# wqk in four transfers with four semaphores, and 24 products of zeros in place of 28

## The chip, the cores and the metric

The kernel runs on one core of a Trainium2 chip: TensorE (matrix products), VectorE, ScalarE, GpSimd, and SyncE (SP), whose queue issues most of the transfers. The metric is the device time of one execution in microseconds, as the median of several runs. Lower is better.

## The reference

Input x has 8 sequences of 512 rows of 256 numbers, in f32. First comes an attention layer that only yields one number for a row, the sum of its exponentials, and a small gate network behind it; then a layernorm; then a mixture of 12 experts, in which each row uses the best 3 in each of two layers; then a layernorm.

```python
q = (x @ Wq.T).astype(bfloat16); k = (x @ Wk.T).astype(bfloat16)
q, k = rope(q), rope(k)
e = where(causal, exp(q @ k.T / 16), 0)
o = relu(e.sum(-1) @ fc1_w.T + fc1_b) @ fc2_w.T + fc2_b
x = layernorm(x + o)
xa = x @ P_w.T;  C1, C2, C3 = softmax of the top 3 of xa @ U.T, for three U
h = gelu(sum_e C1[:, e] * (x @ W1[e].T))
y = sum_e C2[:, e] * (h @ W2[e].T) + C3 @ b2
x = layernorm(x + y)
```

## The kernel before

Every engine has its own hand-written program, and semaphores order them. The work has two stages.

The first stage goes over the rows in 8 chunks of 512 (four sequences of 128 rows each). For each chunk TensorE makes four projections, numbers g = 0 to 3: two halves of q and two of k. A projection (`project`, L767 to L776) multiplies the part `wqk[:, k, g, :]` by the transposed chunk, in f32, over two halves k; each of its two products is shown as two MATMUL records in the trace, so a projection has four. Two banks take turns, so projection n waits for the copy of projection n - 2 (L771). ScalarE copies each projection out of its bank (`qk_copy`, L561), VectorE turns it by the rope (L1078 to L1086), TensorE makes the scores of the chunk before (L786, L788), ScalarE takes exponentials and their sums (L571). Between these, parts of the second stage are prepared: the split of the experts' weights into two f16 halves, the first layernorms and the routing of the first rows. The split needs the largest absolute value of each weight array: VectorE takes that of w1T (L1092), ScalarE sums the absolute values of w2T in three parts (`w_sum`, L578). The first of these sums stands in ScalarE's program behind chunk 1, ahead of the copies of chunk 2, and waits for both parts of w2T (L577).

The second stage goes over 32 tiles of 128 rows with the experts' products (L935), most of the run's length.

At the start, GpSimd clears `zeros`, and TensorE makes `WARM` products of it that nobody reads (L957 to L958), waits for wqk (L959) and enters the loop over chunks. `project(c, 0)` also waits for its chunk's two transfers (L770). After `project(0, 1)` TensorE waits for all six small constant loads (L965) and makes the product of the routing matrices (L967).

Transfers: SP's queue issues, in this order, chunk 0 of x transposed (two transfers, L329), the routing matrices (L342, L343), chunk 1, b2 (L345), w1T in two parts (L338, L339), chunk 2, w2T in two parts (L338, L339), chunk 3, and later the rest and x's own rows (L334). ScalarE's queue issues wqk as one transfer (L548), then, behind a wait for GpSimd's clearing and one small Exp that loads its table (L550), the constants `cb`, `identf`, `iota12`, `gatew` (L551 to L554). Chunk 0 lies in memory in runs of 128 numbers (512 bytes), wqk as one transfer in runs of 4 KB for a partition.

Of the kernel before, what the change touches and what calls it, by code (L numbers as in the profile page):

```python
# [81 lines left out]
def build(nc, x, xT, wqkT, gate, fc2, p_w, uT, w1T, w2T, b2e, constb, constf, out):  # L82
    ctx = ExitStack()
    with ctx:
        def sb(name, shape, dt):
            return ctx.enter_context(nc.sbuf_tensor(name, shape, dt))
# [4 lines left out]
        def sem(name):  # L91
            return ctx.enter_context(nc.semaphore(name))
# [12 lines left out]
        wqk = sb("wqk", [P, NC, 4, P], F32)  # L105
# [69 lines left out]
        RING, HT = 4, 4  # L175

        LAST_SCORE = (HGT, MISC)
        WARM = 28
        Z = GT * NR * NE
        KEPT = 10  # L180

        ld_qk = sem("ld_qk")
        ld_const = sem("ld_const")
        ld_rows = sem("ld_rows")
        ld_b2 = sem("ld_b2")
# [81 lines left out]
        def wait(eng, s, value):  # L267

            if value > 0:
                eng.wait_ge(s, value)  # L270
# [7 lines left out]
        for i in range(NT + 2):  # L278
            order = [(i - 2, 1, j) for j in range(experts_of(i - 2))] if i >= 2 else []
            order += [(i, 0, j) for j in range(experts_of(i))] if i < NT else []  # L280
            for key in order:
                slot[key] = len(taker)
                act = key[1] == 0 and key[2] == 0
# [101 lines left out]
        def _(pool):  # L385
# [69 lines left out]
            def select_of(g):  # L455
                pool.wait_ge(ids_done, g + 1)
                pool.wait_ge(C_done, g + 1)
                _, v = nc.values_load_multi_w_load_instructions(
                    ids[0:1, g, :, :].rearrange("p m r -> p (m r)"), engines=[ENGINE.Pool], min_val=0, max_val=NE,
                    skip_runtime_bounds_check_because="an id is a sum of one-hot entries times 1..12")  # L460
                t = slice(max(GT * g, 1), GT * (g + 1))
                for m in range(NM):
                    for j in range(TOPK):
                        c = pool.tensor_copy(Csel[:, t, m, j:j + 1], C[:, t, m, bass.ds(v[REC * m + j], 1)])
                c.then_inc(csel_done, 1)
# [79 lines left out]

        @block.scalar
        def _(act):
            act.dma_start(wqk[:, :, :, :], wqkT).then_inc(ld_qk, 16)  # L548
            act.wait_ge(zero_done, 3)
            act.activation(warm[:, :], minus_half[0:1, 0:1], ACT.Exp)  # L550
            act.dma_start(cb[:, :], constb).then_inc(ld_const, 16)  # L551
# [214 lines left out]
        def _(pe):  # L766
            def project(c, g):  # L767
                n = 4 * c + g
                if g == 0:
                    pe.wait_ge(ld_seq[c % 4], 32 * (c // 4 + 1))  # L770
                wait(pe, qk_copied, n - 1)  # L771
                for k in range(NC):
                    mm = pe.matmul(bank[PROJ[n % 2]][:, :], wqk[:, k, g, :],  # L773
                                   xTb[:, c % 4, k, :, :].rearrange("p s n -> p (s n)"),
                                   start=(k == 0), stop=(k == NC - 1))
                mm.then_inc(proj_done, 1)  # L776
# [171 lines left out]
            def load_ids(g):  # L948
                pe.wait_ge(ids_done, g + 1)
                _, v = nc.values_load_multi_w_load_instructions(  # L950
                    ids[0:1, g, :, :].rearrange("p m r -> p (m r)"), engines=[ENGINE.PE], min_val=0, max_val=NE,
                    skip_runtime_bounds_check_because="an id is a sum of one-hot entries times 1..12")
                held_ids[g] = v


            pe.wait_ge(zero_done, 1)
            for n in range(WARM):  # L957
                pe.matmul(bank[SCORE[n % 2]][:, 0:DIM], zeros[:, 0:P], zeros[:, :], start=True, stop=True)  # L958
            pe.wait_ge(ld_qk, 16)  # L959
            for c in range(NCH):  # L960
                project(c, 0)
                early_aux(c, 0, early)
                project(c, 1)
                if c == 0:
                    pe.wait_ge(ld_const, 16 * 6)  # L965
                    for k in range(NC):
                        mm = pe.matmul(bank[MISC][:, k * NR * NE:(k + 1) * NR * NE], pws[:, k, :], uTs[:, :],  # L967
                                       start=True, stop=True)
                    mm.then_inc(M_done, 1)
                if c == 3:  # L970
                    peak_transpose()
                early_aux(c, 1, early)
                if c:
                    scores(c - 1, 0)
                project(c, 2)
                early_aux(c, 2, early)
                if c:
                    scores(c - 1, 1)
                project(c, 3)
                if c == 3:  # L980
                    peak_spread()
                early_aux(c, 3, early)
                if c:
                    gate_transpose(c - 1)
# [503 lines left out]
```

## Time and profile before

| | us |
|---|---|
| median of 3 runs | 300.6 |
| lowest and highest | 300.32, 302.5 |
| the profiled execution's own time | 304.48 |
| its span, first to last instruction | 302.5 |
| TensorE products busy | 271.4 (90%) |
| VectorE busy | 248.2 (82%) |
| ScalarE busy | 164.1 (54%) |
| GpSimd busy | 144.3 (48%) |

Times in the rows are microseconds from the span's start. A busy TensorE is not one at its peak, since products overlap in the records. "PEld" is the load of the stationary operand. "SPq" and "ACTq" are the queues of SP and ScalarE, on which transfers are issued. Idle time in brackets is that of the engine just ahead of the row, with what ended it.

### The profile page before, as it was taken

Reading aid. Unit: us, or ns where it says so; the run is one execution under the profiler, and the core shown is the slowest. Engines: PE = TensorE matmul, PEld = TensorE weight load, DVE = VectorE, ACT = ScalarE, POOL = GpSimd, SP = SyncE. Lnnn points to the kernel's source line nnn. Section 1 sums busy time; section 2 is a strip of 40 time slices with the busy share of each in tenths; the row PEclk is TensorE's granted clock in tenths of the full one; section 3 lists DMA queues with packets and bytes.
Section 4 is the critical chain, followed back from the end, with each engine's and each line's share of the span. In section 5 each row is a group of like instructions: output and inputs, shape, how many; then the busy total and the mean of one; then the engine's idle time right before and its main releaser. Section 6 shows DMA issues by size and latency. Waiting matters only on the chain.

```text
span 302.5 us, 6418 instructions
## 1 busy us (share of the span) xinstructions
PE 271.4 (90%) x2028; PEld 196.4 (65%) x2030; DVE 248.2 (82%) x728; ACT 164.1 (54%) x341; POOL 144.3 (48%) x315
## 2 busy tenths in 40 slices
PE   7997999997959974999999999999999999999980
PEld 5443444553526663797877877777778878788960
DVE  0368498999966985879999999999999989987872
ACT  1246745765736446036746846837846946545430
POOL 0200006999998752432482383374364362474421
PEclk9999899999979995799999999999999999999997
DMA  8997999970000000001001001000100101010111
GB/s 234 419 386 265 165 190 202 144 101 0 0 1 2 1 2 0 0 2 37 20 20 36 20 18 32 23 20 21 31 25 18 37 20 36 20 35 22 36 35 39
DMA packets 19211, 20.50 MB, mean 68 GB/s; under 512 B 1620, under 2 KB 18408, under 8 KB 18664
## 3 DMA queue, kind: packets, MB, share of 16 engines
q1 hardware_dynamic: 18456, 19.13, 26.7%
q10 hardware_dynamic: 720, 0.93, 1.0%
q8 instruction: 18, 0.29, 0.4%
q14 instruction: 17, 0.14, 0.1%
HBM read 15.83 MB, written 4.19 MB: 66 GB/s over the span
## 4 chain that ended last, share of the span: by engine, by line
PE 57%; DVE 24%; issue 7%; SPq 4%; DMA 4%; ACT 2%; POOL 0%; DVEq 0%; POOLq 0%
PE bank L935 37%; PE bank L773 8%; DVE early L1303 7%; DMA W<-in_w2T 4%; PE bank L821 4%; SPq L338 2%; DVE early L1360 2%; DVE xsin L1079 2%; PE bank L786 2%; DVE top L1172 2%; DVE zrest L1187 2%; PE bank L832 2%; DVE st L1355 1%; DVE x1T L1162 1%; DVE xcos L1078 1%
## 5 line engine op out<-in xcount | busy, mean ns | idle before, releaser
L935 PE MATMUL bank<-W,early 128*128 (+1 forms) x630 | 75.7, 276 | 5.3 <-DVE early L1360 5.3
L935 PE MATMUL bank<-W,x1T 128*128 (+1 forms) x630 | 74.9, 273 | 0.6 <-DVE early L1303 0.3
L935 PEld LDWEIGHTS bank<-W,early 128*128 128x128 f16 x630 | 60.3, 99 | 17.1 <-DVE early L1360 7.0
L935 PEld LDWEIGHTS bank<-W,x1T 128*128 128x128 f16 x630 | 59.8, 98 | 11.3 <-issue 2.5
L1303 DVE SCALAR_TENSOR_TENSOR early<-bank,Csel,early 128x256 f32<-128x256 f32 x124 | 59.7, 482 | 8.1 <-PE bank L935 3.7
L773 PE MATMUL bank<-early,wqk 128*128 128x512 f32 x128 | 63.2, 627 | 2.8 <-ACT qk L561 1.9
L773 PEld LDWEIGHTS bank<-early,wqk 128*128 128x128 f32 x128 | 23.2, 197 | 24.3 <-issue 21.8
L682 ACT ACTIVATE early<-early 128x256 f32<-128x256 f32 x32 | 13.3, 417 | 45.1 <-DVE early L1303 44.9
L561 ACT ACTIVATE qk<-bank 128x512 bf16<-128x512 f32 x32 | 18.9, 594 | 34.3 <-PE bank L773 34.2
L519 POOL TENSOR_SCALAR ve<-mv 128x1 f32<-128x1 f32 x32 | 7.3, 227 | 60.5 <-DVE mv L1356 59.9
L1078 DVE TENSOR_TENSOR xcos<-qk,cb 128x1024 bf16<-128x1024 bf16 x16 | 11.9, 746 | 20.3 <-ACT qk L561 20.2
L732 ACT ACTIVATE early<-bank,ipow 128x256 f16<-128x256 f32 x32 | 15.0, 468 | 19.6 <-PE bank L1029 19.4
L427 POOL TENSOR_TENSOR xs<-early,x 128x512 f32<-128x512 f32 x16 | 20.4, 1273 | 4.8 <-ACT early L623 4.8
L742 ACT ACTIVATE early<-early,shift,rstd 128x256 f32<-128x256 f32 x32 | 18.9, 589 | 6.8 <-POOL shift L521 6.8
L419 POOL TENSOR_SCALAR ve<-mv 128x4 f32<-128x4 f32 x8 | 2.6, 330 | 40.3 <-DVE mv L1155 40.2
L411 POOL TENSOR_TENSOR W<-wtmp,W 128x512 f16<-128x512 f32 x16 | 21.1, 1316 | 1.4
L571 ACT ACTIVATE expd<-bank 128x128 bf16<-128x128 f32 (+3 forms) x32 | 13.7, 436 | 10.4 <-PE bank L788 10.4
L520 POOL TENSOR_TENSOR rstd<-ve,minus_half 128x1 f32<-128x1 f32 x32 | 18.0, 561 | 2.7
L821 PE MATMUL bank<-fc2s,hgT 32*128 32x256 f32 x64 | 19.0, 417 | 0.3 <-ACT early L623 0.3
L610 ACT ACTIVATE x<-xs,shift,rstd 128x256 f32<-128x256 f32 x32 | 17.3, 591 | 1.8 <-POOL xs L427 1.8
L1360 DVE SCALAR_TENSOR_TENSOR early<-bank,ipow,early 128x256 f16<-128x256 f32 x32 | 14.5, 454 | 3.5 <-ACT early L732 3.5
L677 ACT ACTIVATE early<-bank,Csel 128x256 f32<-128x256 f32 x31 | 14.6, 471 | 4.1 <-PE bank L935 3.8
(117 smaller groups left out, 453.6 us busy)
## 6 DMA issues: line engine op xcount, KB each, us to landing
early<-in_xT SPq DMA_DIRECT2D x16, 256.0 KB, 7.2
xs<-in_x SPq DMA_DIRECT2D x32, 128.0 KB, 7.8
out<-early SPq DMA_DIRECT2D x32, 128.0 KB
W<-in_w1T SPq DMA_DIRECT2D x1, 2048.0 KB, 11.8
W<-in_w2T SPq DMA_DIRECT2D x1, 2048.0 KB, 12.5
W<-in_w1T SPq DMA_DIRECT2D x1, 1024.0 KB, 7.1
W<-in_w2T SPq DMA_DIRECT2D x1, 1024.0 KB, 14.1
wqk<-in_wqkT ACTq DMA_DIRECT2D x1, 512.0 KB, 3.7
```

What stands on the lines that cost most here:

```text
L411: pool.tensor_tensor(W[:, m, e + 1, 1, :], wtmp[:, n % 2, :], W[:, m, e + 1, 0, :], ALU.subtract)\
L427: pool.tensor_tensor(xs[:, t:t + 2, :].rearrange("p t d -> p (t d)"), brows[:, h, :], x1[:, g % 3, 2 * h:2 * h + 2, :].rearrange("p t d -> ...
L520: link(pool.tensor_tensor(rstd2[:, p:p + 1], ve2[:, p:p + 1], minus_half[:, 0:1], ALU.pow))
L561: act.activation(qk[:, c % 2, g, :, :].rearrange("p s n -> p (s n)"), bank[PROJ[n % 2]][:, :], ACT.Copy)\
L610: n = act.activation(x1[:, g % 3, t, :], xs[:, GT * g + t, :], ACT.Identity, bias=shift[:, g % 2, t:t + 1], scale=rstd[:, g % 2, t:t + 1])
L732: act.activation(hT[:, t % 2, 0, :, :].rearrange("p c n -> p (c n)"), bank[HT][:, 0:DIM], ACT.Copy, scale=ipow2[:, 1:2]).then_inc(hhi_done, 1)
L742: act.activation(y[:, t % 4, :], y[:, t % 4, :], ACT.Identity, bias=shift2[:, p:p + 1], scale=rstd2[:, p:p + 1]).then_inc(y_done, 1)
L773: mm = pe.matmul(bank[PROJ[n % 2]][:, :], wqk[:, k, g, :], xTb[:, c % 4, k, :, :].rearrange("p s n -> p (s n)"), start=(k == 0), stop=(k = ...
L821: mm = pe.matmul(bank[ROWS][:, t % 2 * DIM:(t % 2 + 1) * DIM], hgT[PAD * T:PAD * (T + 1), u, :, :].rearrange("p b r -> p (b r)"), fc2s[PAD ...
L935: mm = pe.matmul(where[:, 0:DIM], lhs(hx, c), w, start=(k == 0), stop=(k == 5))
L1303: dve.scalar_tensor_tensor(sums, bank[place[n]][:, 0:DIM], c, before, ALU.mult, ALU.add)\
L1360: dve.scalar_tensor_tensor(hT[:, t % 2, 1, :, :].rearrange("p c n -> p (c n)"), bank[HT][:, 0:DIM], ipow2[:, 1:2], hT[:, t % 2, 0, :, :].r ...
```

## The change

wqk is loaded in four transfers, one for each projection g, each with its own semaphore; in chunk 0 each projection waits for its own part; the one wait ahead of the loop is gone. The products of zeros go from 28 to 24. A part is `wqkT[:, :, g, :]`, runs of 128 numbers (512 bytes).

```diff
-        WARM = 28
+        WARM = 24
-        ld_qk = sem("ld_qk")
+        ld_qk = [sem(f"ld_qk{g}") for g in range(4)]
         def _(act):
-            act.dma_start(wqk[:, :, :, :], wqkT).then_inc(ld_qk, 16)
+            for g in range(4):
+                act.dma_start(wqk[:, :, g, :], wqkT[:, :, g, :]).then_inc(ld_qk[g], 16)
             act.wait_ge(zero_done, 3)
             def project(c, g):
                 n = 4 * c + g
+                if c == 0:
+                    pe.wait_ge(ld_qk[g], 16)
                 if g == 0:
                     pe.wait_ge(ld_seq[c % 4], 32 * (c // 4 + 1))
             for n in range(WARM):
                 pe.matmul(bank[SCORE[n % 2]][:, 0:DIM], zeros[:, 0:P], zeros[:, :], start=True, stop=True)
-            pe.wait_ge(ld_qk, 16)
```

## Rows read from the trace of the kernel before

**Rows 1.** The chain that ended last, in order of time: start, length, what

```profile
7.19 6.55 SPq L338
13.78 12.47 DMA W<-in_w2T
...
28.96 3.43 PE bank L773 x4
32.97 1.79 PE bank L773 x4
```

**Rows 2.** Timeline, 0 to 14: start, length, engine, line, operation

```profile
0.74 0.43 ACTq L548 DMA_DIRECT2D wqk<-in_wqkT  x1
1.10 5.34 PE L958 MATMUL bank<-zeros 128*128 128x256 bf16 x28 [1.10 <-POOL zeros L394]
2.77 0.60 ACTq L554 DMA_DIRECT2D gatew<-in_gate  x1
7.38 3.67 PE L773 MATMUL bank<-early,wqk 128*128 128x512 f32 x8 [0.94 <-DMA early<-in_xT]
9.38 0.60 ACT L561 ACTIVATE qk<-bank 128x512 bf16<-128x512 f32 x1 [6.68 <-PE bank L773]
10.99 0.63 PE L967 MATMUL bank<-uTs,pws 64*128 64x36 f32 x4
```

**Rows 3.** Transfers: from, to, queue, KB each, us from issue to landing

```profile
wqk<-in_wqkT ACTq DMA_DIRECT2D x1, 512.0 KB, 3.7
gatew<-in_gate ACTq DMA_DIRECT2D x1, 1.0 KB, 5.6
```

**Rows 4.** Timeline, ScalarE, 22 to 30

```profile
26.28 1.91 ACT L578 ACTIVATE junk<-W 128x2048 bf16<-128x2048 f32 x1 [2.10 <-DMA W<-in_w2T]
```

**Rows 5.** Timeline, TensorE, four places

```profile
23.17 3.60 PE L773 MATMUL bank<-early,wqk 128*128 128x512 f32 x8
...
28.96 2.58 PE L773 MATMUL bank<-early,wqk 128*128 128x512 f32 x3 [1.86 <-ACT qk L561]
...
86.91 0.38 PE L786 MATMUL bank<-x1T,qr 128*128 128x512 bf16 x1 [3.10 <-DVE x1T L1086]
...
115.93 0.59 PE L883 MATMUL bank<-b2s,C3T 72*128 72x256 bf16 x2 [4.19 <-issue]
```

**Rows 6.** Stretches: PE, PEld, DVE, ACT, POOL busy; granted clock, DMA share, GB/s

```profile
6.44:7.38 0.94, 0.00 (x1) 0.03 (x1) 0.00 (x0) 0.00 (x0) 0.00 (x0) 1.00 1.22 244
7.38:27.10 19.72, 19.71 (x66) 9.25 (x66) 12.34 (x20) 7.28 (x18) 2.09 (x4) 1.00 1.05 391
...
29.35:32.77 3.42, 3.42 (x10) 1.39 (x9) 2.06 (x4) 2.73 (x8) 0.00 (x0) 0.50 0.94 156
32.77:40.00 7.23, 7.10 (x23) 3.07 (x20) 4.42 (x7) 4.55 (x11) 0.00 (x0) 1.00 1.18 205
...
87.38:90.79 3.41, 3.41 (x7) 1.53 (x6) 1.18 (x3) 1.86 (x5) 3.16 (x5) 0.50 0.01 2
...
114.69:124.93 10.24, 7.48 (x32) 4.91 (x33) 6.58 (x24) 5.23 (x10) 3.80 (x10) 0.50 0.00 0
```

**Rows 7.** TensorE: products of zeros from 5.73; all of L958 (ns min/median/max)

```profile
5.73 0.71 PE L958 MATMUL bank<-zeros 128*128 128x256 bf16 x5
...
L958 PE MATMUL bank<-zeros x28: 272/417/417, 1.1 to 6.2; 128*128 128x256 bf16 x28
```

**Rows 8.** DMA queues; windows 1.7:4.4, 2.5:3.9, 3.9:4.3, 4.3:5.3, 12:15; q10 ScalarE's, q1 SP's

```profile
q10 hardware_dynamic: 145, 0.53, 65.4%
...
q10 hardware_dynamic: 112, 0.42, 84.2%
...
q1 hardware_dynamic: 251, 0.13, 105.9%
...
q10 hardware_dynamic: 129, 0.32, 80.0%
...
q1 hardware_dynamic: 78, 1.28, 100.0%
```

## The prediction

> **What bounds the kernel now.** I read the chain that ended last first. TensorE's work is most of it later on, but its early part is a transfer. In order of time it starts on SP's queue, where the issue of the first part of w2T stands 6.55 us, goes on with the 12.47 us that the second part needs to land, and reaches TensorE only through ScalarE [rows 1]. The reader should see what isn't on it: neither wqk, nor chunk 0 of x, nor one of the first chunk's projections.
>
> Next I read the first 12 us. The 28 products of zeros run from 1.10 to 6.44; then TensorE is idle for 0.94 us and the first projection starts at 7.38. What released it was in_xT, chunk 0 of x [rows 2]. wqk was issued at 0.74 and took 3.7 us, so it was there at 4.4, about 3 us before that [rows 2, 3]. The wait that the change splits is thus not one that ended last; it can help only through the order in which the DMA engines serve their two queues.
>
> Then I read the place where chain and front meet. ScalarE has nothing left to do at 24.18 (26.28 - 2.10), is idle for 2.10 us until w2T is there, takes the sum of its absolute values (L578, 1.91 us) and only then copies the next two projections [rows 4]. TensorE runs out of work at 27.10 and is idle for 1.86 us until 28.96, behind those copies [rows 5]. From 7.38 to 27.10 it was never idle [rows 6]: the front is a solid block of TensorE work that ends against w2T's landing. TensorE could come 1.86 us later and still be in time; if it comes earlier, it waits longer.
>
> **The change part by part.** *Four fewer products of zeros.* Five of the last ones take 0.71 us at the high clock, one of them 0.272 by itself, so one follows the other by (0.71 - 0.27) / 4 = 0.11 us [rows 7]. Four fewer end the block 0.44 us sooner, at 6.0. That by itself only lengthens the idle time before the first projection, since x comes after. The clock is the cover to watch: products that took 417 ns in the beginning took 272 at the end, and the five that begin at 5.73 are numbers 24 to 28 [rows 7], so with 24 the clock is up before the block ends; and it did not fall over the 0.94 us of idle time behind it [rows 6]. I put this at nothing; were the clock down in the first projections, four products would take 1.64 us more (3.43 for 1.79) [rows 1], and the idle time at 27.10 would hide that too.
>
> *Four waits on TensorE.* Each stands ahead of one projection of chunk 0, and the whole of TensorE's order is queued behind it. Eight records of projections take 3.60 us [rows 5], so a projection, which is four of them, takes 1.8 us; one issue on ScalarE's queue took 0.43 us [rows 2], so the parts start about that far apart. Unless a part lands over 1.8 us later than the one ahead of it, only the first wait can count. Nothing.
>
> *Three more issues on ScalarE's queue.* The issues of cb and of the three small loads, and ScalarE's table load behind them, move back by some 3 x 0.43 = 1.3 us. ScalarE's first copy waits 6.68 us for a projection [rows 2], which covers this. The last of the constants was issued at 2.77 and took 5.6 us: there at 8.4 [rows 2, 3]. With 1.3 us more it is there at 9.7, later if its packets now meet chunk 1's. The product that needs it (L967) ran at 10.99 [rows 2] and would run at about 10.2 if the front moves up as below. Were it late by some tenths, the 1.86 us of idle time at 27.10 would take that up.
>
> *What chunk 0 gains.* cb's 0.32 MB took 80.0% of the engines from 4.3 to 5.3, about 0.8 us, while chunk 0's second half stood [rows 8]. Now cb comes behind four wqk parts on its queue, whose packets (512-byte runs in place of 4 KB) take turns with those of x, not whole 4 KB ones. So chunk 0 lands about 0.8 us sooner, and the first projection starts at 6.6 instead of 7.38. Bounds: no gain, if the same bytes are ahead of it; 1.4 us, if x is there when the products of zeros end at 6.0. I take 0.8. **It is worth nothing at the end**: the place where it goes is the wait at 27.10, which becomes longer by as much.
>
> *What w2T loses.* This is the term that counts. SP's queue is served in order, and the engines are busy all the time from 6.44 to 27.1 (mean shares of 1.22 and then 1.05) [rows 6], and two queues keep them so from about 2.5 on (80.0% to 105.9% by one queue alone) [rows 8], so any engine time that wqk costs more delays w2T by as much. Before, ScalarE's queue took 65.4% of 2.7 us, 1.77 us of all engines, for its first 0.53 MB [rows 8]; in the stretch where x was also flowing, 84.2% of 1.4 us, 1.18 us for 0.42 MB, which makes 1.47 us for wqk's 0.524 MB. Chunk 0, whose runs have the size that wqk's will have, moved 0.13 MB in 105.9% of 0.4 us, 0.31 MB per us: 1.71 us for 0.524 MB. The large runs of the experts' weights moved 1.28 MB in 3.0 us, 0.43 MB per us: 1.23 us. So the new wqk costs 1.71 - 1.77 = -0.06 us at best, 1.71 - 1.23 = +0.48 at worst by those rows, and if it went at the 205 GB/s of the 128 KB loads of x at 33 to 40 [rows 6], 2.56 - 1.77 = +0.79. Those loads write in a different way (16 partitions, 1 KB runs); the nearest row is chunk 0's, and the nearest old price that of the stretch shared with it: 1.71 - 1.47 = +0.24 us, which I take.
>
> A rule is against that price: the Trainium skill, page "DMA: Bandwidth & Descriptors", section Specifications, gives 512 B as the smallest transfer at line rate. By it the term is 0 and the time that of before. The rows don't agree in full: 0.31 MB per us in 512-byte runs against 0.43 in large ones.
>
> **Sum.** On the path: products of zeros 0, waits 0, constants 0, front -0.8 x 0, w2T +0.24. The profiled execution took 304.48 us (span 302.5), so 304.72; by the same difference the median of 300.6 becomes 300.84. Range of this case alone: -0.06 to +0.79 around 300.6, with 0.3 us on either side (so far does the lowest run shown lie under the median), 300.2 to 301.7.
>
> **Rivals.** *The front's gain gets through.* If in an execution without the profiler w2T landed over 2 us sooner against TensorE, the wait at 27.10 would not be there and 0.8 us (at most 1.4) come off: 299.8 (299.2). For it: the profiled execution is 3.9 us longer than the median. Against it: the chain of waits goes through w2T with 1.86 us to spare, and the transfer's length is engine time, which no wait on the compute engines makes.
>
> *A second stretch at the low clock (slower).* TensorE's idle time at 27.10 grows from 1.86 to 1.86 + 0.8 + 0.24 = 2.9 us. After 1.86 us the granted clock fell to half (1.2 of 2.4 GHz) at 29.35 and stayed there for 3.42 us [rows 6]; four products took 3.43 us instead of 1.79 [rows 1], so a second stretch costs 1.64 us. In a later place a wait of 3.10 us gave one stretch of 3.41 us, and one of 4.19 us (111.74 to 115.93) a stretch of 10.24 [rows 5, 6]. It decides somewhere between 3.1 and 4.2 us of idle time; 2.9 lies nearer to the single stretch. Time: 300.84 + 1.64 = 302.5, with the worst w2T term 303.0.
>
> *The change doesn't do what it says.* Chunk 0 lands when it did, TensorE is idle from 6.0 to 7.38 and no projection starts sooner: 300.84 all the same, as w2T alone sets the end.
>
> **How the numbers follow.** Forecast (front sooner, absorbed by w2T) 0.62; nothing sooner, same time, 0.11; gain gets through 0.10; second low stretch 0.17. Predicted 300.8. For 8 in 10 the range must hold both outer cases in their likelier part: from 299.2 to 303.0. One per cent, 3.0 us, is about what a measurement here can tell from no change. The gain would have to be joined by the loss of the half-clock stretch (-1.64) to come near -3: faster 0.03. The slower case needs the worst w2T term and more: 0.06. Same 0.91.
>
> **What would show it.** Right: the first projection at 6.2 to 7.0; the products of zeros end at 6.0; ScalarE's idle time before L578 grows to about 3.1 us, that of TensorE behind it to 2.9; L578 starts within 26.2 to 27.1; the chain still passes w2T. Wrong: L578 starts before 26, or no wait of ScalarE for w2T; a granted half clock for longer than 3.4 us around 30; the first projection at 7.38; a wait of L967 or of a part of wqk in the list of waits. What would make it wrong is above all w2T's landing: each us there is one at the end.

## The result, and the profile after

The changed kernel takes 306.99 us (median of 4 runs, 305.41 to 309.45) where the kernel before took 301.36 in the same comparison: a ratio of 1.0193, 95% interval 1.0111 to 1.0275. It is slower, and outside the range of the prediction. Ratios, here and below, leave out executions more than 1.5% above the fastest of their kernel (four of ten in e8_sum_later, two of ten in e2_small_first, one of ten in e13_consts_first_sum_later, one of the kernel before in each of two comparisons).

The profiled execution of the changed kernel has a span of 304.7 us. Its chain that ended last, in order of time (start, length, what), no longer begins with w2T:

```profile
5.01 11.95 DMA gatew<-in_gate
17.00 1.07 PE bank L969 x4
18.07 8.62 PE bank L776 x16
37.22 1.79 PE bank L776 x4
41.86 2.30 DVE amaxp L1094
```

A load of 1 KB, gatew, stands where the 2 MB of w2T's second part stood before [rows 1]. The timeline of the first 17 us (start, length, engine, line, operation, idle time ahead of it):

```profile
0.75 2.62 ACTq L549 DMA_DIRECT2D wqk<-in_wqkT  x4
1.10 4.24 PE L961 MATMUL bank<-zeros 128*128 128x256 bf16 x24 [1.10 <-POOL zeros L394]
5.01 0.52 ACTq L555 DMA_DIRECT2D gatew<-in_gate  x1
5.21 3.67 PE L776 MATMUL bank<-early,wqk 128*128 128x512 f32 x8
...
17.00 1.07 PE L969 MATMUL bank<-uTs,pws 64*128 64x36 f32 x4 [8.12 <-DMA gatew<-in_gate]
```

The first projection starts at 5.21, right behind the products of zeros, against 7.38 [rows 2]: that part of the change does what it says, 2.2 us of it. Chunk 0 allows it, as the slower of its two transfers takes 3.8 us to land, against 6.0 before. That the products of zeros end as soon as 5.3 is partly luck: 24 of them took 4.24 us here, and in runs described below 4.09 (e5_own_wait) and 5.30 (e4_zeros_24, e8_sum_later); in e8 the first projection starts at 6.20. Then, after two projections, TensorE stands for 8.12 us ahead of L969 (L967 before), which ran at 10.99 and now runs at 17.00. The list of waits says whom else that holds up:

```profile
DVE xcos L1080 <- DMA gatew<-in_gate: 17.0, 1, 17.0
...
PE bank L969 <- DMA gatew<-in_gate: 8.1, 1, 8.1
```

The transfers of ScalarE's queue behind wqk, from issue to landing:

```profile
cb<-in_constb ACTq DMA_DIRECT2D x1, 323.2 KB, 5.4
...
identf<-in_constf ACTq DMA_DIRECT2D x1, 64.0 KB, 5.5
...
iota<-in_constf ACTq DMA_DIRECT2D x1, 6.0 KB, 7.7
gatew<-in_gate ACTq DMA_DIRECT2D x1, 1.0 KB, 11.9
```

The smallest takes longest: gatew took 5.6 us before [rows 3]. What its packets met is seen in the queues (packets, MB, share of 16 engines; q1 is SP's queue, q10 ScalarE's), first from 9.7 to 17, then from 9.7 to 12 alone:

```profile
q1 hardware_dynamic: 651, 2.96, 99.4%
q10 hardware_dynamic: 159, 0.00, 1.4%
...
q1 hardware_dynamic: 114, 1.00, 105.2%
q10 hardware_dynamic: 120, 0.00, 3.4%
```

ScalarE's queue had 159 small packets left and used 1.4% of the engines; the rest went to SP's queue, w1T first. iota12 and gatew are 128 runs each, one for a partition, so eight of each for an engine if they are spread evenly. If each of the sixteen waits for one packet of weights, it is the weights' pace that counts: 0.43 MB per us over 16 engines [rows 8], that is 0.3 us for 8 KB and 0.6 us for 16 KB, 5 to 10 us for sixteen (an estimate from these rows). The Trainium skill, page "DMA: Bandwidth & Descriptors", section Queues, rings and completion order, has the rule: an engine takes turns between the queues that have work, a packet at a time. The trace agrees: from 9.7 to 12, while both queues had work, they moved 114 and 120 packets, near one for one. The 159 took 7.3 us, within the estimate.

The clock paid too. Stretches of busy time (PE, PEld, DVE, ACT, POOL; then granted clock, DMA share, GB/s):

```profile
10.94:17.00 6.06, 0.00 (x0) 0.00 (x0) 0.02 (x1) 0.00 (x0) 1.73 (x4) 0.50 1.01 407
17.00:21.18 4.18, 4.18 (x8) 2.44 (x9) 2.50 (x6) 0.00 (x0) 0.00 (x0) 0.50 1.13 409
```

The clock fell at 10.94, some 2 us into the idle time, and TensorE works at half clock, 1.2 GHz, until 21.18. From there it is never short of work, and ScalarE starts the first sum over w2T without a wait:

```profile
32.10 1.89 ACT L579 ACTIVATE junk<-W 128x2048 bf16<-128x2048 f32 x1
...
39.47 1.88 PE L776 MATMUL bank<-early,wqk 128*128 128x512 f32 x4
```

The second row is the first projection of chunk 3, the milestone used below. Before, it started at

```profile
35.02 1.45 PE L773 MATMUL bank<-early,wqk 128*128 128x512 f32 x3
```

so the loss at the milestone is 39.47 - 35.02 = 4.45 us. It is made up of 6.0 us at L967 and 2.0 more by the half clock up to 21.18, together 8.0 at the seventh projection, here in the changed kernel and in the kernel before:

```profile
26.86 1.94 PE L776 MATMUL bank<-early,wqk 128*128 128x512 f32 x4
...
18.85 1.94 PE L773 MATMUL bank<-early,wqk 128*128 128x512 f32 x4
```

Of these the wait for w2T that is gone gave back 1.86 us, and the half clock behind it some 1.6 [rows 1, 5, 6]. The two profiled spans differ by 2.2 us only, because the executions differ later: the kernel before has half clock for 3.41 us at 87.38 and for 10.24 at 114.69 [rows 6], the changed kernel none near 90 and this stretch:

```profile
120.16:126.99 6.83, 5.89 (x25) 3.82 (x26) 4.17 (x14) 2.77 (x7) 3.72 (x10) 0.50 0.00 0
```

The profiled execution of e4_zeros_24 below, the kernel before with 24 products, is like the changed kernel's in this (none near 87, 6.82 us at 115.61); its milestone is 34.96 and its span 300.3, and 304.7 - 300.3 is again 4.4. The medians differ by 5.6 us; those of the kernel before may mix such executions with others in which the half clock at 29 does not come, where the milestone is at 33.38 (e1_gate_late's trace, the same up to gatew), 6.1 us ahead.

### The profile page after: what moved, and what is told of

Its sections match the earlier page's. It is cut to its first block, busy times and chain, and to the rows that moved or that the text cites. A ratio compares the mean times of both kernels' runs of the same rounds, so it can differ in the third digit from the quotient of the medians.

```text
span 304.7 us, 6415 instructions
## 1 busy us (share of the span) xinstructions
PE 268.2 (88%) x2024; PEld 195.2 (64%) x2026; DVE 247.6 (81%) x728; ACT 164.4 (54%) x341; POOL 145.5 (48%) x315
## 3 DMA queue, kind: packets, MB, share of 16 engines
HBM read 15.83 MB, written 4.19 MB: 66 GB/s over the span
## 4 chain that ended last, share of the span: by engine, by line
PE 50%; DVE 33%; issue 8%; DMA 4%; ACT 2%; ACTq 1%; POOL 1%; DVEq 0%; POOLq 0%
PE bank L938 28%; PE bank L776 12%; DVE early L1305 11%; DMA gatew<-in_gate 4%; DVE early L1362 3%; DVE st L1357 2%; DVE xsin L1081 2%; PE bank L824 2%; PE bank L789 2%; DVE top L1174 2%; DVE stats L1153 2%; DVE zrest L1189 2%; DVE x1T L1164 2%; DVE xcos L1080 2%; PE bank L835 1%
## 5 line engine op out<-in xcount | busy, mean ns | idle before, releaser
L938 PEld LDWEIGHTS bank<-W,x1T 128*128 128x128 f16 x630 | 60.0, 98 | 11.1 <-issue 2.5
L776 PE MATMUL bank<-early,wqk 128*128 128x512 f32 x128 | 61.8, 615 | 0.0
L683 ACT ACTIVATE early<-early 128x256 f32<-128x256 f32 x32 | 13.3, 416 | 44.9 <-DVE early L1305 44.7
## 6 DMA issues: line engine op xcount, KB each, us to landing
W<-in_w2T SPq DMA_DIRECT2D x1, 2048.0 KB, 12.4
```

The lines of the kernel that those rows point to most:

```text
L776: mm = pe.matmul(bank[PROJ[n % 2]][:, :], wqk[:, k, g, :], xTb[:, c % 4, k, :, :].rearrange("p s n -> p (s n)"), start=(k == 0), stop=(k = ...
L938: mm = pe.matmul(where[:, 0:DIM], lhs(hx, c), w, start=(k == 0), stop=(k == 5))
```

## The experiments

Theory A: the wait for the late small constants is the cause. B: the split of wqk itself, by w2T. C: the clock, through fewer products of zeros. Ratios are against the kernel before on the same chip.

**Only gatew, a little later.** In the kernel before:

```diff
+            act.wait_ge(ld_qk, 16)
             act.dma_start(gatew[:, :], gate).then_inc(ld_const, 16)
```

> The kernel before, with one edit: ScalarE's queue issues gatew (1 KB) only once wqk has landed, at about 4.5 us instead of 2.8. wqk stays one transfer, 28 products of zeros. Theory A (the small constants are the cause: issued later, their packets meet those of the experts' weights, and TensorE waits for them before L967): gatew lands at 12 to 17 instead of 8.4, L967 starts then, and the run is 3 to 6 us slower than the kernel before. Theory B (the split of wqk costs the time, by w2T landing later): no change, 300 to 302.5. Theory C (fewer products of zeros, the clock): no change.

0.9997 (0.9952 to 1.0041): no change, against A's numbers. gatew was issued at 4.46 and took 5.2 us, there at 9.7, and L968 was as before:

```profile
10.99 0.63 PE L968 MATMUL bank<-uTs,pws 64*128 64x36 f32 x4
```

1.7 us later is not yet late, and chunk 1's packets of 512 bytes, which it met, held it up little.

**gatew later still, beside w1T.** In the kernel before:

```diff
+            act.wait_ge(ld_seq[0], 32)
             act.dma_start(gatew[:, :], gate).then_inc(ld_const, 16)
```

> The kernel before, with one edit: ScalarE's queue issues gatew only once chunk 0 has landed (about 7.3 us), so its 8-byte packets reach the engines together with the first part of w1T (8 KB packets from 8.3 on). wqk stays one transfer. Theory A: gatew lands at 13 to 18, L967 waits 3 to 7 us for it, the run is 2 to 5 us slower than the kernel before (304.5 to 308). If packets of weights don't hold up the small ones: gatew lands at about 9.5, no change.

1.0195 (1.0119 to 1.0272), the whole loss of the change, with wqk in one transfer and 28 products; the milestone is at 39.51. Issued at 7.38, gatew took 8.9 us:

```profile
16.29 1.07 PE L968 MATMUL bank<-uTs,pws 64*128 64x36 f32 x4 [5.13 <-DMA gatew<-in_gate]
```

Between 4.46 and 7.38 lies the step: whether its packets pass before w1T's reach the engines. The changed kernel, with 5.01, is past it.

**Two small constants first.** In the changed kernel, iota12 and gatew ahead of the parts of wqk:

```diff
+            act.dma_start(iota12[:, :], constf[:, P:P + NE]).then_inc(ld_const, 16)
+            act.dma_start(gatew[:, :], gate).then_inc(ld_const, 16)
             for g in range(4):
...
-            act.dma_start(iota12[:, :], constf[:, P:P + NE]).then_inc(ld_const, 16)
-            act.dma_start(gatew[:, :], gate).then_inc(ld_const, 16)
```

> The changed kernel, with iota12 and gatew (6 KB and 1 KB) issued ahead of the four parts of wqk instead of behind cb and identf. Theory A: gatew lands before 9, L967 waits at most some 2 us for identf, and the time is back at that of the kernel before, 299.5 to 302.5. Theory B: wqk still in 512-byte runs, still slow, 305 to 308. Theory C: still 24 products, still slow.

1.0058 (1.0004 to 1.0113): not back. A expected at most 2 us of waiting for identf; the wait has only changed its name, to identf, whose 128 runs now come last and took 11.1 us:

```profile
16.15 1.06 PE L969 MATMUL bank<-uTs,pws 64*128 64x36 f32 x4 [6.72 <-DMA identf<-in_constf]
```

The milestone of this execution is at 38.95, 0.5 us ahead of the changed kernel's; why the ratio is so much smaller is not shown.

**Weights held until the constants are there.** In the changed kernel:

```diff
+            sp.wait_ge(ld_const, 16 * 6)
             load_experts(0, w1T)
```

> The changed kernel, with SP's queue holding w1T (and all that is behind it) until all six constants have landed. Theory A (what holds up the small packets is the weights' large ones on the same engines): gatew lands at about 8 to 9.5 instead of 15 to 17, L967 does not wait; w2T lands 0.5 to 2 us later, which TensorE pays: 302 to 305. If the small transfers are late for the four parts of wqk ahead of them, they land at 14 to 17 as before and the time is above 307.

gatew took 5.5 us again, issued at 5.05, and L970 ran at 10.61, so it is the weights that held it up. But w2T came at 31.1, and the time is 1.0216 (1.0124 to 1.0308), more than the 302 to 305 expected:

```profile
10.61 0.63 PE L970 MATMUL bank<-uTs,pws 64*128 64x36 f32 x4 [1.21 <-DMA gatew<-in_gate]
...
31.13 1.91 ACT L580 ACTIVATE junk<-W 128x2048 bf16<-128x2048 f32 x1 [7.33 <-DMA W<-in_w2T]
```

**The number of products, both ways.** In the changed kernel and in the kernel before:

```diff
-        WARM = 24
+        WARM = 28
```

> The changed kernel with 28 products of zeros again. Theory C (the clock falls or rises late for lack of them): back to 300 to 302.5, no half clock behind the front. Theories A and B: as the changed kernel, 305 to 309; L967 still starts at about 17.

1.0163 (1.0064 to 1.0262), L969 at 14.66: slow as the changed kernel.

```diff
-        WARM = 28
+        WARM = 24
```

> The kernel before with 24 products of zeros and nothing else. Theory C: slower by 2 to 6 us. Theories A and B: within 1 per cent of the kernel before; the idle time ahead of the first projection grows from 0.94 to about 1.4 us and the clock holds.

0.9999 (0.9962 to 1.0035), idle time 0.85 us ahead of the first projection. C falls in both directions.

**All four constants first.** In the changed kernel, the issues of cb, identf, iota12 and gatew moved ahead of the parts of wqk.

> The changed kernel, with all four constants of ScalarE's queue (cb, identf, iota12, gatew) issued ahead of the four parts of wqk. Theory A: the constants land by 8.5, ahead of the weights' large packets, L967 does not wait for them, the first projection starts later than in the changed kernel (6.5 to 8.5). Theory D (the runs of wqk make w2T late): w2T still lands at 27 to 28.5 and the time is 303 to 306. Theory E (order): w2T lands by 26.8, time within 1 per cent of the kernel before.

1.0035 (0.9987 to 1.0083): the loss is gone, with wqk still split. The first projection starts at 7.50 (it waits 2.06 us for wqk), L969 does not wait, w2T is there at 26.86:

```profile
26.86 1.91 ACT L579 ACTIVATE junk<-W 128x2048 bf16<-128x2048 f32 x1 [0.84 <-DMA W<-in_w2T]
```

**A wait for what L967 reads, alone.** Transfers as in the changed kernel; each group of constants gets its own semaphore (ScalarE's wait behind its first two copies moves to its gate work in the same way):

```diff
-                    pe.wait_ge(ld_const, 16 * 6)
+                    pe.wait_ge(ld_mat, 16 * 2)
...
+                if c == 1:
+                    pe.wait_ge(ld_cb, 16)
                 if c:
                     scores(c - 1, 0)
...
+                if c == 1:
+                    pe.wait_ge(ld_const, 16 * 3)
                 if c:
                     gate_transpose(c - 1)
...
-            dve.wait_ge(ld_const, 16 * 6)
+            dve.wait_ge(ld_cb, 16)
```

> The changed kernel with the wait ahead of L967 narrowed: the routing matrices (which L967 reads) get a semaphore, cb gets one (VectorE's rope and TensorE's scores wait for it), and identf, iota12 and gatew keep the old one, which ScalarE and TensorE wait for only ahead of the gate's work of chunk 0. Transfers and their order stay as in the changed kernel. Theory A (the wait for late small constants is the whole loss): the small ones still land at 14 to 17, nobody waits for them, L967 runs at about 9, TensorE again waits for w2T behind ScalarE (idle time of 3 to 5 us near 27), and the time is within 1 per cent of the kernel before, 301 to 304 where that has 302.8. Theory B (wqk in 512-byte runs costs the time otherwise): still 305 to 308.

1.0143 (1.0064 to 1.0223), so A as a whole account falls. gatew still landed late and nobody waited. The loss moved to w2T, in the way of the prediction's slower rival:

```profile
28.20 1.91 ACT L581 ACTIVATE junk<-W 128x2048 bf16<-128x2048 f32 x1 [6.11 <-DMA W<-in_w2T]
...
30.89 3.78 PE L778 MATMUL bank<-early,wqk 128*128 128x512 f32 x4 [5.89 <-ACT qk L564]
...
27.70:34.53 6.83, 3.64 (x5) 1.39 (x6) 2.06 (x4) 5.49 (x10) 0.00 (x0) 0.50 0.93 138
...
37.04 1.88 PE L778 MATMUL bank<-early,wqk 128*128 128x512 f32 x4
```

w2T is there 1.9 us later than before (28.20 against 26.28 [rows 4]), TensorE stands for 5.89 us, and the half clock lasts 6.83 us instead of 3.42. The milestone, 37.04, is 2.0 us behind.

**Shorter runs of wqk as the reason?** As e5, with a part of wqk as one run of 1 KB for a partition:

```diff
-        wqk = sb("wqk", [P, NC, 4, P], F32)
+        wqk = sb("wqk", [P, 4, NC, P], F32)
...
-                act.dma_start(wqk[:, :, g, :], wqkT[:, :, g, :]).then_inc(ld_qk[g], 16)
+                act.dma_start(wqk[:, g, :, :], wqkT[:, g, :, :]).then_inc(ld_qk[g], 16)
...
-                    mm = pe.matmul(bank[PROJ[n % 2]][:, :], wqk[:, k, g, :],
+                    mm = pe.matmul(bank[PROJ[n % 2]][:, :], wqk[:, g, k, :],
```

> As e5_own_wait, with wqk laid out so that a part is 1 KB in one run for a partition, in memory and on chip, instead of two of 512 bytes (the host hands it over in that order). Theory D (the 512-byte runs of wqk make w2T late, 28.2 us there against 26.3): w2T lands 0.5 us or more sooner than in e5_own_wait, 26.3 to 27.6, and the time falls to 302 to 305. Theory E (not the runs but the order, cb and the small constants beside chunk 1 and w1T): w2T lands at 27.5 to 28.7 as before, time 305 to 307.

w2T at 28.12, 1.0107 (1.0026 to 1.0189). The landing is not what theory D expected, and the time misses it by 0.2 us. With e12, whose runs are of 512 bytes and whose w2T comes at 26.86, D falls as it was forecast. That shorter runs cost some tenths is not excluded: the second part of w2T is issued at 14.46 here and at 14.85 in e5, but at 14.39 in g3, whose runs are of 512 bytes.

**What delays w2T: TensorE's own instructions.** In e5 (and in e10) the queues from 25 to 27.7 have one packet that the kernel before has only from 27 to 29, behind w2T:

```profile
q1 hardware_dynamic: 1067, 0.77, 92.1%
q8 instruction: 1, 0.02, 2.5%
```

2.5% of 16 engines over 2.7 us is 1.08 us on one engine. It appears when TensorE has begun 191 records (products and weight loads) in e5 and 195 in the kernel before, which a sooner front reaches sooner. The count alone does not set the place: in e4 the packet comes at 39.9, at 251 records. So the number of records was changed, at an equal number of columns: in e5, 12 products of zeros of 512 columns in place of 24 of 256:

```diff
-        zeros = sb("zeros", [P, DIM], BF16)
+        zeros = sb("zeros", [P, 2 * DIM], BF16)
...
-        WARM = 24
+        WARM = 12
...
-                pe.matmul(bank[SCORE[n % 2]][:, 0:DIM], zeros[:, 0:P], zeros[:, :], start=True, stop=True)
+                pe.matmul(bank[SCORE[n % 2]][:, :], zeros[:, 0:P], zeros[:, :], start=True, stop=True)
```

> As e5_own_wait, with 12 products of zeros of 512 columns instead of 24 of 256: as long on TensorE, 24 records fewer. Theory F (TensorE's own instruction fetch holds up w2T): the 16 KB packet of queue q8 moves from 25.5 to behind w2T's landing (after 27), w2T lands at 26.8 to 27.3 instead of 28.2, projection 12 starts at 35.5 to 36.3 instead of 37.0, the time falls by 0.5 to 2 us against e5_own_wait (306.6). Theory E alone (order of the transfers): w2T still at 28, time 305 to 308.

and in the kernel before, 56 of 128 columns in place of 28 of 256:

```diff
-        WARM = 28
+        WARM = 56
...
-                pe.matmul(bank[SCORE[n % 2]][:, 0:DIM], zeros[:, 0:P], zeros[:, :], start=True, stop=True)
+                pe.matmul(bank[SCORE[n % 2]][:, 0:P], zeros[:, 0:P], zeros[:, 0:P], start=True, stop=True)
```

> The kernel before, with 56 products of zeros of 128 columns instead of 28 of 256: as long on TensorE, 56 records more, all else as it was. Theory F: the packet of queue q8 comes sooner, at about 18 to 25 instead of 27.5, and delays the part of w1T or w2T that is then on its engine; w2T lands at 26.8 to 27.4 instead of 26.3 and the run is 0 to 2 us slower. Theory E alone: w2T at 26.3, no change.

g2 is the clear one. Nothing but the count and width of products that nobody reads has changed, the first projection starts at 7.46, and it is 1.0104 (1.0051 to 1.0157). From 23 to 26.5 the queue q8 has its packet (19 in the whole execution instead of 18, so it does carry TensorE's instructions), and w2T is there at 27.45 instead of 26.28:

```profile
q8 instruction: 1, 0.02, 1.9%
...
27.45 1.91 ACT L578 ACTIVATE junk<-W 128x2048 bf16<-128x2048 f32 x1 [3.20 <-DMA W<-in_w2T]
...
30.14 3.35 PE L773 MATMUL bank<-early,wqk 128*128 128x512 f32 x4 [2.96 <-ACT qk L561]
```

Its milestone is at 36.19, 1.2 us behind that of before; its median is 2.8 us behind, and the rest was not separated.

In g1 the packet was gone from ahead of w2T, which came 0.9 us sooner than in e5, about as expected; the time was not better, 1.0125 (1.0062 to 1.0189). TensorE still stood long enough for the long half-clock stretch, and that took the 0.9 us back (the first projection of chunk 3 at 37.16):

```profile
27.34 1.91 ACT L581 ACTIVATE junk<-W 128x2048 bf16<-128x2048 f32 x1 [4.90 <-DMA W<-in_w2T]
...
30.02 3.78 PE L778 MATMUL bank<-early,wqk 128*128 128x512 f32 x4 [4.68 <-ACT qk L564]
...
28.77:35.60 6.83, 5.58 (x12) 2.75 (x13) 2.05 (x4) 5.18 (x15) 0.00 (x0) 0.50 1.01 134
```

**Taking w2T's wait off the path.** The three sums over w2T on ScalarE, moved back: in the kernel before (e9), in e5 (e8), in e12 (e13) and in g1 (g3).

```diff
                 if c == 2:
-                    w_sum(1)
+                    w_sum(0)
...
-                if c in (1, 2):
-                    w_sum(2 * (c - 1))
+                if c == 2:
+                    w_sum(1)
+                    w_sum(2)
```

> The kernel before, with only the three sums over w2T moved back on ScalarE as in e8_sum_later (first sum in the middle of chunk 2, the others at its end). wqk one transfer, 28 products. Theory (in the kernel before, w2T's landing at 26.3 sets the end of the first chunks through ScalarE): the wait of 1.9 us of TensorE at 27 goes, and the half clock behind it; projection 12 starts at 31 to 33 instead of 35; 1 to 4 us faster than the kernel before. If ScalarE's sums themselves hold TensorE up wherever they stand: no change.

> As e5_own_wait, and the three sums over w2T on ScalarE moved back: the first from the end of chunk 1 to the middle of chunk 2, the second and third to the end of chunk 2, so that the copies of chunk 2's first two projections no longer stand behind w2T. Theory: the sooner front is absorbed by w2T as the prediction had it; with that wait out of the way it gets through: 2 to 6 us faster than the kernel before (297 to 301), TensorE idle less than 1 us near 27. If something else holds that stage, no faster than e5_own_wait.

> e12_consts_first with the sums over w2T moved back as in e9_sum_later_only: the split of wqk, no late constants, no wait for w2T ahead of chunk 2's copies. Theory: as e9 or better by the sooner front (up to 1 us): 297 to 300 where the kernel before has 301.5. If chunk 0 does not land sooner in this order, no better than e9.

> As e8_sum_later (own semaphores, sums over w2T moved back), with 12 wide products of zeros as in g1_wide_zeros. Theory F: w2T at about 27 instead of 28.7, less idle time of TensorE at the gate's transposes near 31, time 298 to 301.5, at or below e9_sum_later_only's 300.6 where the kernel before has 302 to 303. Theory E alone: as e8, 301 to 303.

| | ratio | interval |
|---|---|---|
| e9: kernel before, sums later | 0.9941 | 0.9896 to 0.9985 |
| e8: own semaphores, sums later | 0.9981 | 0.9927 to 1.0034 |
| e13: constants first, sums later | 0.9977 | 0.9927 to 1.0026 |
| g3: as e8, 12 wide products | 0.9964 | 0.9930 to 0.9998 |

e9's and g3's intervals lie below 1, by 0.6 and 0.4% in the middle; with intervals that overlap, none of the four is shown to be better than another. In e9 TensorE goes through 27 us without a wait:

```profile
24.71 1.88 PE L774 MATMUL bank<-early,wqk 128*128 128x512 f32 x4
...
26.76 1.94 PE L774 MATMUL bank<-early,wqk 128*128 128x512 f32 x4
...
31.27 1.02 PE L774 MATMUL bank<-early,wqk 128*128 128x512 f32 x2
```

The milestone is at 31.27 instead of 35.02. e8 against e5 (0.9981 against 1.0143, on the same chip; medians of all executions 302.98 and 306.64) shows that in e5 it was indeed the copies behind w2T that cost the time. e8 was expected 2 to 6 us below the kernel before and e13 at 297 to 300 (its median is 301.61); both missed.

## Why the prediction was wrong, point by point

**The step that failed is "three more issues on ScalarE's queue".** It moved the last constant by the delay of its issue, 1.3 us, kept its 5.6 us from issue to landing, got 9.7, and left the rest to "some tenths". Two things were off. The four issues took 2.62 us, 0.65 each, not 0.43 (four parts of one run for a partition took 1.87, in e10), so gatew was issued at 5.01, 2.2 us later than before. That alone would not have cost much (e1 has 1.7). What did is that the time to land is not a property of the transfer: it went from 5.6 to 11.9 us, because w1T was now on the engines. The prediction named chunk 1 as what the packets would meet and did not look at what came next on SP's queue, w1T's issue, which stands in the same timeline of the kernel before:

```profile
4.90 0.36 SPq L338 DMA_DIRECT2D W<-in_w1T  x1
```

e6 shows this with one line of the kernel before, e7 by holding w1T back, e12 by the order of the issues.

**The cover that was named was too small.** The 1.86 us at 27.10 were to take up a late constant. They did, and the half clock behind them too; L967 was 6.0 us late, and the half clock of its own idle time made it 8.0.

**Right:** the split wait was not one that ended last; four products fewer cost nothing (e3, e4); chunk 0 came sooner; the sooner front is worth nothing at the end as long as ScalarE waits for w2T (in e5 TensorE runs out of work at 25.0 instead of 27.1 and waits that much longer). Chunk 0's gain was mis-sized: 2.2 us, outside the bound of 1.4. Its slower transfer took 3.8 us instead of 6.0, and the products of zeros ended at 5.3, not at 6.0, which was worked out from one execution; others end at 5.2 to 6.4.

**w2T's term was too small.** +0.24 was forecast, bounded at +0.79. It is +0.8 in the changed kernel (14.72 + 12.4 against 13.78 + 12.5), where nothing waits for it, and +0.6 (e12) to +1.9 (e5) without the wait for constants. One share is there before w2T's second part is issued, in the kernel before and in the changed one at

```profile
13.78 0.43 SPq L339 DMA_DIRECT2D W<-in_w2T  x1
...
14.72 0.43 SPq L339 DMA_DIRECT2D W<-in_w2T  x1
```

and at 14.51 in e12, 14.76 in g1 and 14.85 in e5. It begins in the front, since w1T's first part already lands 0.9 us later (4.83 + 8.1 against 4.90 + 7.1). That engine time spent there delays w2T is what the prediction said; whether the runs of wqk or the order of the small loads costs it stays open. The other share was not foreseen: the fetch of TensorE's instructions, where it falls ahead of w2T's end. From issue to landing w2T's second part takes 13.3 to 13.8 us with it (e5, e7, e8, e10, g2) and 12.3 to 12.8 without it in all other runs but e2 (13.3).

**The slower rival was real, and hidden.** In e5 the idle time is 5.89 us, beyond the 3.1 to 4.2 us from which the rival was to decide, and the half clock lasts 6.83 us. It was priced on an idle time of 2.9; of the 3.0 us more, 1.3 are the front's (2.1 us sooner, not 0.8) and 1.7 w2T's (+1.9, not +0.24). For 2.9 us the prediction was right: 2.96 in g2 brought one stretch of 3.42. But idle time alone does not decide: 3.10 us ahead of 86.91 brought 3.41 us of half clock in the kernel before [rows 5, 6] and 3.12 ahead of 91.21 none in the changed one, and 3.85 us, with 1.27 close behind, brought 6.83 there and 10.24 in e2. The row of 10.24 us that the prediction read for one wait of 4.19 has such a second one, of 1.26, in it. In the changed kernel itself it does not occur, since TensorE is late there. That e5 stays 1.4% slow rests on w2T's delay and on the clock; how much each has was not separated.

**Missed altogether:** no rival had a wait that takes the place of the one removed on the *constants* of the same queue, though L965 waits for all six of them at once and L967 reads two. A wait of L967 stands only among the signs of being wrong, without a price; that sign and another, no wait of ScalarE for w2T, came.

## What to carry to other kernels

A transfer that is issued later does not land later by as much: ask which packets it will meet on the engines, and look for small transfers of many short runs that fall behind a large one's. A wait on a group of loads is as late as its least needed member, so give what is read first its own semaphore, or issue the small loads first. Before making a front sooner, find the wait it runs into; here moving that wait (e9) brought 0.6%, which the sooner front could not.

## What the runs showed of the hardware that was not expected

- gatew, 1 KB in 128 runs, took 5.2 to 5.6 us when it passed ahead of the weights (the kernel before, e1, e7) and 8.9 to 12.4 us beside them (e6, the changed kernel, e5), with the engines 99.4% on the other queue.
- A fetch of 16 KB of instructions takes about 1.08 us on one DMA engine (2.5% of 16 engines over 2.7 us), and a large transfer beside it landed later by as much: with 56 narrow products of zeros in place of 28, at equal columns, w2T was there 1.2 us later and the kernel was 1.0% slower (g2).
- TensorE's granted clock: 1.79 us of idle time near 27 (e1) and 2.03 near 31 (e8) left it at 2.4 GHz, 1.86 and 1.93 us brought half clock for 3.42 us in two others (the kernel before, e4), and 4.68 and 5.89 us brought it for 6.83 us (g1, e5).
